# Four reorderings in a two-block gated cross-attention kernel: a weight subtraction on GpSimd, a context split and a set of bounds on VectorE, query copies on ScalarE

## The chip, the cores and the metric

The kernel runs on one core of a Trainium2 chip. The core has five engines that work side by side and wait for one another through semaphores: PE (TensorE, matrix products; PEld are its weight loads), DVE (VectorE), ACT (ScalarE), POOL (GpSimd) and SP (SyncE, which here issues nearly all DMAs). The metric is the device time of one execution in microseconds (us), as a median of several executions. Three executions of the kernel before gave 1867.23, 1867.36 and 1871.78 us, a median of 1867.36 us.

## The reference

Input are 4 sequences of 256 tokens by 256 features, `x`, and for each a context of 1601 rows by 128 features. Two layers follow one another, and each adds a gated cross-attention and a gated mixture of experts:

```
x = x + tanh(g_xattn[0]) * L0_xattn(layernorm(x), ctx)   # 16 heads of 16, layernorm on q and k, biases
x = x + tanh(g_ffn[0])   * L0_ffn(layernorm(x))          # 32 experts, top 8, capacity
x = x + tanh(g_xattn[1]) * L1_xattn(layernorm(x), ctx)   # 16 heads of 128, rmsnorm on q and k
x = x + tanh(g_ffn[1])   * L1_ffn(layernorm(x))          # 64 experts, top 4, router, 2 shared experts

# L1_xattn, for each batch element
q = rmsnorm(x @ Wq, gq); k = rmsnorm(ctx @ Wk, gk); v = ctx @ Wv      # heads of 128
out = softmax(q k^T / sqrt(128)) v;  out @ Wo
```

All is fp32. Products that need it are made from a high part, rounded to the fast fp32r format, and a low part, the exact remainder: three fast products (high-high, high-low, low-high) stand for one full one. So a tensor is often handled twice, as a "hi" copy (mostly ACT) and a "lo" subtraction (mostly DVE or POOL).

## The kernel before, in words

Every engine has its own instruction stream, written by hand in program order; nothing is reordered by a scheduler. An engine executes its stream strictly in order, and a wait holds everything behind it. `me.do(...)` makes an engine wait for its own instruction before the next; `.then_inc(s.name, 1)` raises a semaphore at the end and `wait_ge` waits for one. `primed(...)` only adds a constant.

The four stages are the first cross-attention (until about 380 us in the trace), the first experts (until about 610 us), the second cross-attention (until about 1545 us) and the second experts. The change touches the first and the third.

First cross-attention. Before the first scores, DVE scales the keys (L1778), makes the constants for the exponentials from the weights (`bounds()`, L1735 to L1741, six operations on a few columns, at whose end `bound0_ready` is raised), then subtracts the low parts of the first two key tiles (`read_keys(0, 0, 0)` and `(0, 0, 1)`, L1822), then turns to the first queries (`read_queries(0, 0)`, L1840 to L1845), and then to key tiles 2 and 3. After tile 1 it raises `kst_ready`, on which SP issues 12 DMAs of a first part of the keys (L604), and after tile 3 again, for 12 of the second part. PE waits for these DMAs before its first scores (L1235), and ACT for the scores and for `bound0_ready` before its first exponential (L972). POOL meanwhile works on L771, L775 and L778.

Second cross-attention. A preparation comes first: the products Wv Wo of all heads (PE L1394, `m1`), whose high parts ACT copies (L1022) and whose low parts are taken by POOL for heads 0 to 7 in one instruction over 2048 columns (L840, from the copy `m1w` that ACT makes in L1026) and by DVE for the rest (L2091). Beside it DVE normalizes x (L1665, eight tiles), PE turns the tiles (L449, "the token turn", `ln_turned`), ACT and DVE copy them out (L358, L1671), and PE goes on with the queries (L1420). POOL also clears the sums `rk1` and `acc1` (L842, L843), after the turn, and raises `sums_zeroed`.

Then come four batches (b = 0 to 3). Each has a key phase and a head phase. In the key phase the low part of the transposed context is subtracted on DVE over 1601 columns (L2103, `ctxT_lo`), while POOL subtracts and adds on the untransposed one (L856 to L861). PE makes the queries (L1420), then 52 key tiles in the order of `KINDS` ("k": L1404, squared by ACT in L1069, summed by DVE in L2131; "g": L1470, copied by ACT in L1073, weighted by POOL in L871, summed by DVE in L2131). PE may be four tiles ahead of ACT. DVE sums the squares of the queries (L2139, L2140), ACT takes the root behind the fourth tile (L1076), DVE inverts it (L2149), POOL scales the queries (L851, two instructions), and PE turns them (L1455) at the sixteenth tile. Between batches 1 and 2 the half of x that is finished is updated on DVE (`update`: L1962, L1638, L1641, and `variance`: L1652); this stands at the start of batch 2, ahead of L2103.

At the end of the key phase DVE finishes the sums of squares (L2163, `k1_var`), ACT takes their root (L1093) and loads the table of exponentials (L1094), DVE inverts (L2166, `rk1_ready`), and ACT begins the exponentials (L1112) of the first pair of heads. Around this stand the four high copies of the second query tile (ACT `split_products`, L1056) and their four low parts (DVE `low_products`, L2122): one copy ahead of the root, three behind the table load. Each pair of heads then runs over 13 context tiles: scores (PE L1404), exponentials (ACT L1112, two per tile), split (ACT L1120 or DVE L2206, then DVE L2210), sums (DVE L2219), values (PE L1404). PE may issue the scores of tile t once the exponentials of tile t-2 are done (t-3 for the first three).

## Time and profile before

| | |
|---|---|
| median of three executions | 1867.36 us (1867.23 to 1871.78) |
| profiled execution, own time | 1871.98 us |
| its span | 1870.2 us |
| busy in the span | PE 1785.2 us (95%), DVE 1403.3 us (75%), ACT 1231.6 us (66%), POOL 485.5 us (26%) |
| mean granted TensorE clock | 0.98 |
| busy PE, 380 to 400 us / 800 to 1500 us | 17.06 of 20 us / 684.60 of 700 us |

Times in the trace are counted from the start of the span. An engine's share of busy time tells little about what a change of order is worth; that is read from the places where an engine stands idle and from what ended the idle time. In a timeline row the columns are the start, the time from the first start to the last end of the merged instructions, the engine, the line, the operation, out<-in, the shape, the count, and in brackets the idle time before it and who ended it.

### The profile page before, as it was taken

To read this page: it belongs to the slowest core of one execution; us is meant where nothing else is said; L and a number is where in the kernel's file an instruction comes from. 1 tells how busy PE (TensorE), PEld (TensorE's weight loads), DVE (VectorE), ACT (ScalarE), POOL (GpSimd) and SP (SyncE) were. 2 spreads that over 40 slices of the span, in tenths; PEclk is the share of its full clock that TensorE was granted. 3 is DMA by queue.
4 is the path that set the end of the run, shared out by engine and by line. 5 is a ranking of instruction groups with operands and counts; after the bars stand their busy time and mean duration, and the time that the engine had idled before them with its cause. 6 is when DMAs were issued, how large, how long until landed. Compare 5 with 4: busy or idle time off the path is not lost.

```text
span 1870.2 us, 31883 instructions
## 1 busy us (share of the span) xinstructions
PE 1785.2 (95%) x9201; PEld 1309.9 (70%) x9204; DVE 1403.3 (75%) x2298; ACT 1231.6 (66%) x2094; POOL 485.5 (26%) x425
## 2 busy tenths in 40 slices
PE   5799999999999899999999989999999999999998
PEld 3344444468888667776777767777677777888887
DVE  7566666466666788887888989889789997566665
ACT  4576868842323688888888868888888885222322
POOL 3010101215453650005400054000530102445442
PEclk9899999989999999999999999999999999999999
DMA  3413222345443100000000000000000000554452
GB/s 99 111 46 83 67 62 59 70 175 127 118 111 77 54 18 1 0 0 18 18 1 0 0 18 19 0 0 0 1 22 1 8 9 17 116 116 109 109 116 75
DMA packets 109736, 95.90 MB, mean 51 GB/s; under 512 B 72820, under 2 KB 94200, under 8 KB 109016
## 3 DMA queue, kind: packets, MB, share of 16 engines
q1 hardware_dynamic: 109656, 94.88, 20.4%
q8 instruction: 45, 0.74, 0.2%
q14 instruction: 35, 0.29, 0.0%
HBM read 72.94 MB, written 1.44 MB: 40 GB/s over the span
## 4 chain that ended last, share of the span: by engine, by line
PE 81%; DVE 12%; ACT 3%; issue 2%; SPq 1%; DMA 0%; DVEq 0%; ACTq 0%
PE ps L1404 32%; PE ps L495 17%; PE ps L507 8%; PE ps L1248 5%; PE ps L1235 5%; DVE s_rk L2131 3%; PE ps L1173 3%; PE ps L1420 2%; PE ps L1498 1%; PE ps L1470 1%; PE ps L1526 1%; SPq L604 1%; DVE s_rq L2139 1%; ACT s_p L1112 1%; PE ps L1428 1%
## 5 line engine op out<-in xcount | busy, mean ns | idle before, releaser
L1112 ACT ACTIVATE s_p<-ps,s_g,s_rk 128x256 f32<-128x256 f32 (+1 forms) x832 | 412.5, 560 | 8.8 <-DVE s_dsum L2219 6.6
L1404 PE MATMUL ps<-s_qq,s_ctxT 128*128 (+3 forms) x1248 | 359.6, 402 | 9.6 <-ACT s_p L1112 7.8
L495 PE MATMUL ps<-s_xT,s_wgus 128*128 128x512 f32 x1440 | 348.5, 390 | 0.0
L1404 PE MATMUL ps<-s_ps,s_ctx 128*128 128x512 f32 x1152 | 327.4, 397 | 0.9 <-DVE s_ps L2210 0.9
L495 PEld LDWEIGHTS ps<-s_xT,s_wgus 128*128 128x128 f32 x1440 | 269.7, 188 | 59.6 <-issue 1.5
L2210 DVE TENSOR_TENSOR s_ps<-s_p,s_ps 128x512 fp32r<-128x512 f32 x384 | 269.0, 700 | 20.8 <-ACT s_ps L1120 17.4
L972 ACT ACTIVATE s_p<-ps,s_bsm 128x1024 f32<-128x1024 f32 x208 | 222.6, 1114 | 91.0 <-PE ps L1248 56.9
L1404 PEld LDWEIGHTS ps<-s_qq,s_ctxT 128*128 128x128 f32 (+1 forms) x1248 | 227.0, 186 | 68.2 <-issue 9.5
L1404 PEld LDWEIGHTS ps<-s_ps,s_ctx 128*128 128x128 f32 x1152 | 217.4, 189 | 57.5 <-DVE s_ps L2210 4.2
L2219 DVE TENSOR_TENSOR s_dsum<-s_dsum,s_p 128x512 f32<-128x512 f32 (+1 forms) x352 | 242.0, 687 | 16.5 <-ACT s_p L1112 12.9
L393 ACT CAST s_hs<-s_hw 128x512 fp32r<-128x512 f32 x120 | 74.5, 621 | 197.7 <-DVE s_hw L1995 197.7
L1120 ACT CAST s_ps<-s_p 128x512 fp32r<-128x512 f32 x288 | 179.4, 623 | 33.6 <-PE ps L1404 11.1
L2000 DVE TENSOR_TENSOR s_hs<-s_hw,s_hs 128x512 fp32r<-128x512 f32 x120 | 138.0, 1150 | 80.5 <-ACT s_hs L393 80.5
L507 PE MATMUL ps<-s_hs,s_wds 128*128 128x512 f32 x720 | 185.6, 393 | 1.8 <-DVE s_hs L2000 1.8
L387 ACT ACTIVATE s_sg<-ps 128x512 f32<-128x512 f32 x120 | 71.8, 599 | 145.6 <-PE ps L495 145.6
L1235 PE MATMUL ps<-s_qz,s_kT 96*128 96x512 f32 x416 | 148.1, 458 | 12.3 <-DMA s_kT<-s_kst 8.2
L507 PEld LDWEIGHTS ps<-s_hs,s_wds 128*128 128x128 f32 x720 | 134.7, 188 | 32.0 <-DVE s_hs L2000 2.6
L856 POOL TENSOR_TENSOR s_ctx<-s_stage,s_ctx 128x1536 fp32r<-128x1536 f32 x4 | 15.4, 3855 | 526.5 <-ACT s_ctxw L1039 526.5
L2131 DVE TENSOR_REDUCE s_rk<-s_ksq 128x4 f32<-128x512 f32 x208 | 128.3, 676 | 19.6 <-POOL s_ksq L871 16.4
L1991 DVE TENSOR_TENSOR s_hh<-s_sg,s_wB 128x512 f32<-128x512 f32 x112 | 77.6, 693 | 77.1 <-ACT s_sg L387 75.3
L1248 PE MATMUL ps<-s_p,s_vg 128*32 128x256 f32 x1792 | 126.2, 389 | 2.6 <-DVE s_oT L1850 2.6
L871 POOL TENSOR_TENSOR s_ksq<-s_ksq,s_stage 128x512 f32<-128x512 f32 (+1 forms) x104 | 111.4, 1091 | 35.2 <-ACT s_ksq L1073 34.6
(282 smaller groups left out, 2320.1 us busy)
## 6 DMA issues: line engine op xcount, KB each, us to landing
s_wB<-w1s SPq DMA_DIRECT2D x64, 256.0 KB, 3.9
s_kT<-s_kst SPq DMA_DIRECT2D x96, 128.0 KB, 2.4
s_kT<-s_kst SPq DMA_DIRECT2D x96, 80.0 KB, 2.1
s_wB<-w0s SPq DMA_DIRECT2D x15, 384.0 KB, 3.5
s_wB<-w0s SPq DMA_DIRECT2D x16, 256.0 KB, 3.8
s_wgu<-in_L_ffn_Wg_dram SPq DMA_DIRECT2D x64, 64.0 KB, 2.9
s_wgu<-in_L_ffn_Wu_dram SPq DMA_DIRECT2D x64, 64.0 KB, 2.6
s_wd<-in_L_ffn_Wd_dram SPq DMA_DIRECT2D x64, 64.0 KB, 2.5
```

The source lines that it names most:

```text
L495: ins = nc.tensor.matmul(ps[:, 4 + g, :], WGUS[f][:, slot, w, g, k, :], XT[f][:, x_, k, n], start=c == 0, stop=c == len(ops) - 1)
L507: ins = nc.tensor.matmul(ps[:, 2 * half + k, :], WDS[f][:, slot, w, k * P:(k + 1) * P], hs[:, j % 2, h, :], start=False, stop=False, skip_ ...
L972: nc.scalar.activation(p0[:, n % 4, :], ps[:, 2 * (n % 3):2 * (n % 3) + 2, :].rearrange("p a n -> p (a n)"), ACT.Exp, bias=bsm[:, col:col ...
L1112: ins = nc.scalar.activation(p1[0:r, SLOT1[t], j, :], ps[0:r, BANK1[t], j * SQ:(j + 1) * SQ], ACT.Exp, bias=g1[0:r, 3:4], scale=rk_col(t, ...
L1120: nc.scalar.copy(ps1[:, SPLIT1.index(t) % RING1, 0, :], p1[:, SLOT1[t], :, :].rearrange("p a n -> p (a n)")).then_inc(s.p_hi, 1)
L1235: ins = nc.tensor.matmul(ps[:, 2 * (n % 3) + i, :], kT0[0:32 * COPIES, g, i, t * P:(t + 1) * P], qz[0:32 * COPIES, g % 2, i, :], start=Tru ...
L1248: ins = nc.tensor.matmul(ps[32 * h:32 * h + 32, SUMBANK, dca * SQ:dca * SQ + SQ], vg[:, b % 2, t + dca, c:c + 2 * D0], p0[:, n % 4, h * SQ ...
L1404: ins = nc.tensor.matmul(out, lhs(x_), rhs(y_), start=first and n == 0, stop=last and n == 2)
L2000: v.tensor_tensor(hs[:, j % 2, 1, :], hw[:, j % 2, :], hs[:, j % 2, 0, :].bitcast(F32), ALU.subtract).then_inc(s.hs_lo, 1)
L2131: v.tensor_reduce(rk1[0:ROWS1[u], u, 4 * q:4 * q + 4], lengths(kind, i, u).rearrange("p (h d) -> p h d", h=4), AX, ALU.add).then_inc(s.k1_ ...
L2210: v.tensor_tensor(lo, whole(t), hi.bitcast(F32), ALU.subtract).then_inc(s.p_lo, 1)
L2219: v.tensor_tensor(dsum[0:r, :], dsum[0:r, :], whole(t)[0:r, :], ALU.add).then_inc(s.summed, 1)
```

## The change

On POOL, the subtraction over 2048 columns moves behind the wait for the token turn and the two memsets. On DVE, `bounds()` moves behind the first queries, and the context's low part moves ahead of the update and the variance (which concerns batch 2 alone, since the update is done there only). On ACT, two of the three late query copies move ahead of the root, and the last one behind the first pair of exponentials.

```diff
--- POOL
             g_.tensor_tensor(lo, whole, hi.bitcast(F32), ALU.subtract).then_inc(s.wk_lo, 1)
+            pool.wait_ge(s.ln_turned, 48)
+            me.do(g_.memset(rk1[:], 1.0))
+            g_.memset(acc1[:], 0.0).then_inc(s.sums_zeroed, 1)
             pool.wait_ge(s.m1_read, 4)
             n = slice(0, H1 * D // 2)
             g_.tensor_tensor(m1[:, 1, n], m1w[:], m1[:, 0, n].bitcast(F32), ALU.subtract).then_inc(s.m1_rest, 1)
-            pool.wait_ge(s.ln_turned, 48)
-            me.do(g_.memset(rk1[:], 1.0))
-            g_.memset(acc1[:], 0.0).then_inc(s.sums_zeroed, 1)
--- ACT
-                split_products(TB * b + 1, 0)
+                for j in range(3):
+                    split_products(TB * b + 1, j)
                 act.wait_ge(s.k1_var, b + 1)
                 nc.scalar.activation(rk1[:], rk1[:], ACT.Sqrt, scale=1.0 / D1).then_inc(s.k1_std, 1)
                 nc.scalar.activation(rq1[0:1, 1, 0:1], ones[0:1, 0:1], ACT.Exp).then_inc(s.act_steps, 1)
-                for j in range(1, 4):
-                    split_products(TB * b + 1, j)
...
                         ins.then_inc(s.probs1, 1)
+                        if t == 0 and first:
+                            split_products(TB * b + 1, 3)
--- DVE
             scale_keys(0, 1)
-            bounds()
             read_keys(0, 0, 0)
             read_keys(0, 0, 1)
             dve.wait_ge(s.kf_made, 4)
             dve.sem_inc(s.misc_read, 4)
             read_queries(0, 0)
+            bounds()
             read_keys(0, 0, 2)
...
             for b in range(B):
+                if b == 0:
+                    dve.wait_ge(s.sums_zeroed, 1)
+                else:
+                    dve.wait_ge(s.probs1, primed(KT * 8 * b))
+                dve.wait_ge(s.ctxT_hi, b + 1)
+                v.tensor_tensor(ctxT1[:, 1, 0:KV], stage[:, 0:KV], ctxT1[:, 0, 0:KV].bitcast(F32), ALU.subtract).then_inc(s.ctxT_lo, 1)
                 if b == B // 2:
                     update(acc1[:, 0:4, :].rearrange("p t n -> p (t n)"), 1, 0, 0)
                     variance(range(4))
-                if b == 0:
-                    dve.wait_ge(s.sums_zeroed, 1)
-                else:
-                    dve.wait_ge(s.probs1, primed(KT * 8 * b))
-                dve.wait_ge(s.ctxT_hi, b + 1)
-                v.tensor_tensor(ctxT1[:, 1, 0:KV], stage[:, 0:KV], ctxT1[:, 0, 0:KV].bitcast(F32), ALU.subtract).then_inc(s.ctxT_lo, 1)
```

POOL at the start of the second cross-attention, before and after; `s_m` is `m1`, `s_xn` the sums `acc1`, `s_ctx` the context. Lines shift by one or two in the changed kernel.

```order
L837 TENSOR_TENSOR s_wk<-s_stage,s_wk 128x2x512
L840 TENSOR_TENSOR s_m<-s_m1w,s_m 128x2048
L842 MEMSET s_rk 128x208
L843 MEMSET s_xn 128x2048
L856 TENSOR_TENSOR s_ctx<-s_stage,s_ctx 128x1536
```

```order
L837 TENSOR_TENSOR s_wk<-s_stage,s_wk 128x2x512
L839 MEMSET s_rk 128x208
L840 MEMSET s_xn 128x2048
L843 TENSOR_TENSOR s_m<-s_m1w,s_m 128x2048
L856 TENSOR_TENSOR s_ctx<-s_stage,s_ctx 128x1536
```

The wide subtraction now stands directly ahead of the context work.

ACT at the end of the key phase and the start of the first pair of heads (the same in each batch), before and after; `s_qq` are the query products, `s_rk` the key lengths, `s_p` the exponentials.

```order
L1056 CAST s_qq<-ps 128x4x128
L1093 ACTIVATE s_rk<-s_rk 128x208
L1094 ACT_TABLE_LOAD
L1094 ACTIVATE s_rq<-s_ones 1x1
L1056 CAST s_qq<-ps 128x4x128 x3
L1112 ACTIVATE s_p<-ps,s_g,s_rk 128x256 x2
L1120 CAST s_ps<-s_p 128x512
```

```order
L1056 CAST s_qq<-ps 128x4x128 x3
L1094 ACTIVATE s_rk<-s_rk 128x208
L1095 ACT_TABLE_LOAD
L1095 ACTIVATE s_rq<-s_ones 1x1
L1111 ACTIVATE s_p<-ps,s_g,s_rk 128x256 x2
L1056 CAST s_qq<-ps 128x4x128
L1121 CAST s_ps<-s_p 128x512
```

Two copies went ahead of the root, one behind the first exponentials.

DVE at the start of batch 2, before and after; `s_xn` are the sums, `s_x` is x, `s_ctxT` the transposed context.

```order
L2181 SCALAR_TENSOR_TENSOR s_xn<-ps,s_rd,s_xn 128x256 x4
L1962 SCALAR_TENSOR_TENSOR s_x<-s_xn,s_tg,s_x 128x1024
L1638 BN_STATS s_bn<-s_x 128x6 x4
L1641 BN_AGGR s_mv<-s_bn 128x2 x4
L1652 TENSOR_SCALAR s_lnv<-s_mv 128x4
L2103 TENSOR_TENSOR s_ctxT<-s_stage,s_ctxT 128x1601
L2139 TENSOR_REDUCE s_rq<-s_q1T 128x16
```

```order
L2182 SCALAR_TENSOR_TENSOR s_xn<-ps,s_rd,s_xn 128x256 x4
L2101 TENSOR_TENSOR s_ctxT<-s_stage,s_ctxT 128x1601
L1963 SCALAR_TENSOR_TENSOR s_x<-s_xn,s_tg,s_x 128x1024
L1639 BN_STATS s_bn<-s_x 128x6 x4
L1642 BN_AGGR s_mv<-s_bn 128x2 x4
L1653 TENSOR_SCALAR s_lnv<-s_mv 128x4
L2140 TENSOR_REDUCE s_rq<-s_q1T 128x16
```

The subtraction passed ten instructions of the update and the variance.

## Rows read from the trace of the kernel before

**Rows 1.** Page, part 4: shares of the chain that ended last, by engine
```profile
PE 81%; DVE 12%; ACT 3%; issue 2%; SPq 1%; DMA 0%; DVEq 0%; ACTq 0%
```

**Rows 2.** Timelines: preparation of the second cross-attention, and a normalization without POOL beside it
```profile
12.80 2.67 DVE L1665 TENSOR_SCALAR s_xn<-s_x,s_mv,s_lnv 128x256 f32<-128x256 f32 x8
...
618.04 4.61 DVE L1665 TENSOR_SCALAR s_xn<-s_x,s_mv,s_lnv 128x256 f32<-128x256 f32 x1
...
617.99 4.51 POOL L840 TENSOR_TENSOR s_m<-s_m1w,s_m 128x2048 fp32r<-128x2048 f32 x1 [7.11 <-ACT s_m1w L1026]
...
627.01 1.81 POOL L843 MEMSET s_xn<- 128x2048 f32 x1
...
623.35 3.27 PE L449 MATMUL ps<-s_ident,s_xn 128*128 128x128 f32 x16 [4.25 <-DVE s_xn L1665]
...
627.63 5.31 PE L1420 MATMUL ps<-s_wq,s_xnT 128*128 128x512 f32 x8 [1.02 <-DVE s_xnT L1671]
```

**Rows 3.** Windows: PE, PEld, DVE, ACT, POOL busy us, granted clock, DMA share, GB/s
```profile
624.00:631.00 7.00, 5.97 (x17) 3.33 (x15) 5.63 (x9) 4.36 (x6) 3.42 (x3) 0.51 0.00 0
...
921.00:924.50 3.50, 3.50 (x9) 2.69 (x9) 3.36 (x7) 3.33 (x8) 0.00 (x0) 0.51 0.03 7
...
1098.50:1102.00 3.50, 3.25 (x8) 2.57 (x9) 3.22 (x4) 0.88 (x2) 0.51 (x1) 0.51 0.59 203
```

**Rows 4.** Timelines of batch 0, key phase: POOL, DVE and ACT
```profile
635.26 3.45 POOL L860 TENSOR_TENSOR s_stage<-s_stage,s_ctx 128x1536 f32<-128x1536 f32 x1
...
637.80 0.94 DVE L2110 SCALAR_TENSOR_TENSOR s_g<-s_g 128x1 f32<-128x1 f32 x1
...
642.41 0.21 ACT L1076 ACTIVATE s_rq<-s_rq 128x16 f32<-128x16 f32 x1 [1.08 <-DVE s_rq L2140]
```

**Rows 5.** Timelines of batch 1, start: POOL and DVE
```profile
860.31 3.43 POOL L856 TENSOR_TENSOR s_ctx<-s_stage,s_ctx 128x1536 fp32r<-128x1536 f32 x1 [175.04 <-ACT s_ctxw L1039]
...
861.49 3.94 DVE L2103 TENSOR_TENSOR s_ctxT<-s_stage,s_ctxT 128x1601 fp32r<-128x1601 f32 x1
```

**Rows 6.** Timelines of batch 2, start: DVE, POOL, PE and ACT
```profile
1089.81 3.34 DVE L1962 SCALAR_TENSOR_TENSOR s_x<-s_xn,s_tg,s_x 128x1024 f32<-128x1024 f32 x1
...
1095.03 1.94 DVE L1652 TENSOR_SCALAR s_lnv<-s_mv 128x4 f32<-128x4 f32 x1
1096.89 1.81 DVE L2103 TENSOR_TENSOR s_ctxT<-s_stage,s_ctxT 128x1601 fp32r<-128x1601 f32 x1
1098.62 2.27 DVE L2139 TENSOR_REDUCE s_rq<-s_q1T 128x16 f32<-128x2048 f32 x1
...
1096.91 2.10 POOL L861 TENSOR_TENSOR s_stage<-s_stage,s_ctx 65x128 f32<-65x128 f32 x1
...
1098.76 2.93 PE L1404 MATMUL ps<-s_wk,s_ctxT 128*128 128x512 f32 x6 [4.08 <-DVE s_ctxT L2103]
...
1104.99 0.22 ACT L1076 ACTIVATE s_rq<-s_rq 128x16 f32<-128x16 f32 x1
```

**Rows 7.** Timelines of batch 1, start of the heads: ACT and PE
```profile
916.70 1.51 ACT L1056 CAST s_qq<-ps 128x512 fp32r<-128x512 f32 x3
918.11 1.00 ACT L1112 ACTIVATE s_p<-ps,s_g,s_rk 128x256 f32<-128x256 f32 x2
...
919.26 0.94 PE L1404 MATMUL ps<-s_qq,s_ctxT 128*128 128x512 f32 x3 [1.36 <-ACT s_p L1112]
920.79 2.71 PE L1404 MATMUL ps<-s_qq,s_ctxT 128*128 128x512 f32 x6 [0.59 <-ACT s_p L1112]
```

**Rows 8.** Timelines of the first cross-attention, start: DVE and SP's queue
```profile
44.08 1.53 DVE L1738 TENSOR_SCALAR s_bsm<-s_bsm 128x2 f32<-128x2 f32 x1
...
46.20 1.29 DVE L1822 TENSOR_TENSOR s_kst<-s_p,s_kst 128x512 fp32r<-128x512 f32 x2
...
65.21 0.81 DVE L1810 TENSOR_SCALAR s_kf<-ps,s_wcol 128x512 f32<-128x512 f32 x1 [2.78 <-DMA s_kT<-s_kst]
...
47.52 19.00 SPq L604 DMA_DIRECT2D s_kT<-s_kst  x28
```

More of the change, by code:

```diff
@@ L2092, in _ @@
             for b in range(B):
-                if b == B // 2:
-                    update(acc1[:, 0:4, :].rearrange("p t n -> p (t n)"), 1, 0, 0)
-                    variance(range(4))
                 if b == 0:
@@ L2103, in _ @@
                 v.tensor_tensor(ctxT1[:, 1, 0:KV], stage[:, 0:KV], ctxT1[:, 0, 0:KV].bitcast(F32), ALU.subtract).then_inc(s.ctxT_lo, 1)
+                if b == B // 2:
+                    update(acc1[:, 0:4, :].rearrange("p t n -> p (t n)"), 1, 0, 0)
+                    variance(range(4))
                 if b == 0:
```

## The prediction

> **What bounds the kernel now.** I read the page first. Four fifths of the chain that ended last are PE, an eighth is DVE [rows 1], so a change of order pays only where PE stands idle or where the work that feeds it is late. Then I took the timelines around the four places. At each the reader is to look for the bracket on PE's row, since its releaser says which engine to speed up, and for an instruction of odd length on that engine.
>
> At the preparation PE stands idle for 4.25 us for DVE's normalization, and the reason is one instruction: a tile that takes 4.61 us where eight take 2.67 us elsewhere, 0.33 us each. It starts with GpSimd's 2048-column subtraction (617.99 to 622.50) and ends with it, at 622.65 [rows 2]. Behind the gap TensorE's granted clock is at the lower of its levels, 1.2 GHz, for 7 us [rows 3]. The same blocking is seen in batch 0, where an operation on one column takes 0.94 us and ends with GpSimd's L860 [rows 4], and in batch 1, where the context subtraction (1.81 us alone) takes 3.94 us because L856 holds it up to 863.74 [rows 5, 6]. So: while GpSimd runs a wide subtraction, a DVE operation from SBUF to SBUF waits for its end. It goes both ways: GpSimd's 65-row L861 takes 2.10 us beside L2103 [rows 6].
>
> At batch 2 PE waits 4.08 us for L2103, which stands behind the update; clock at 0.51 from 1098.5 to 1102 [rows 3, 6]. At each start of the heads (four times; batch 1 stands for them) PE waits 1.36 and 0.59 us for exponentials that stand behind three query copies of 1.51 us, and the clock is at 0.51 behind that too [rows 3, 7]. In the first cross-attention SP issues 24 DMAs back to back from the moment `kst_ready` rises, and a DVE operation waits 2.78 us for the last of them [rows 8].
>
> **Part 1, the weight subtraction.** All instructions stay. Without it the eight tiles run 617.7 to 620.4 instead of to 624.6, 4.2 us sooner. PE is free at 619.1, turns, and is done at about 621.2; a copy of 0.69 us later the queries start, at 621.9 instead of 627.63. They also no longer fall into the half clock, which costs up to half of the 5.31 us that the first eight took less their normal share; I take 1.5 us. So PE comes to its first key tile about 7.2 us sooner, at 630.3. But that is not the gain. GpSimd now clears its sums (about 2.1 us with the 1.81 us row, to 623.3), then subtracts for 4.5 us to 627.8. L2103 asks for its turn at 624.3 and is held up until 627.8, ends at 629.5: still in time for PE. GpSimd's L856 (3.43 us) runs behind it to 632.9, L860 (3.45 us) from 633.7 to 637.2. DVE's small `g` operations run into both: the first is free at 632.9, the fourth at 637.2, the fifth behind L861 at 637.7. The query sum L2139 behind them (2.3 us) so ends at 640.1, and ACT's root is at 640.3 instead of 642.41 [rows 2, 4, 5]. ACT stands at that root behind the fourth key tile and PE may be four ahead: it does eight tiles by 635.6 and idles 5.5 us. So the lead is 2.1 us, and PE, which has no gap in the trace from there until 669 us, starts this stretch at half clock. At 3.5 to 7 us of half clock (the two lengths that rows 3 show) of which some passes while it idles, it loses 1.7 to 3.4 us. I take 1.8: **−0.3 us**, from −2.1 (no loss) to +1.3 (all of it).
>
> **Part 2, the third batch's context.** L2103 is asked for at 1089.8, is held up by L856 to 1092.06 (as L1962 was, whose 3.34 us are 2.25 of waiting and 1.1 of work) and ends at 1093.75. PE finds it ready when its queries end at 1094.1 instead of waiting to 1098.76. Behind it DVE does L1962 (1.1 us), the statistics (1.8 us) and L1652, which waits for L860 as before; GpSimd's L860 slips behind L1962 to about 1098.7. L2139 therefore starts at 1098.8, against 1098.62: DVE gains nothing here. But ACT, whose root before stood behind a late fourth tile and a table load of 1.28 us until 1104.99, now has its table loaded and only waits for L2140, at 1101.35: 3.6 us sooner [rows 6]. PE's gap moves too: 1099.4 to 1102.15, some 2.8 us, and a half clock of 3.5 us there costs 1.7 us in a stretch where PE is the bound. The queries scaled by GpSimd hang on DVE's inverse, which comes 2.1 to 2.4 us sooner, a second bound of the same size. **−2.0 us**, from −3.6 (no half clock) to 0 (L860 goes ahead of L1962, all 3.5 us of it).
>
> **Part 3, the bounds.** Before, DVE's constants stand ahead of the key tiles and wait for GpSimd (L1738, two columns, takes from 44.08 to 45.61; the two before it are held up in the same way). Now L1822 takes the first tile between two of GpSimd's operations; GpSimd's last ends at 45.6 plus the 0.65 us of that tile, 46.2, and the second tile is done at 46.85 instead of 47.49: 0.6 us, not 5. The 24 issues (19.00 us for 28, 0.68 each) start and end 0.6 us sooner, and with them the transfer that DVE waits for at 65.21. The bounds themselves are done at about 52.5 (six operations of under 0.2 us without GpSimd beside them, behind the queries at 51.4), before the first exponential could start, at 53.9. The second `kst_ready` comes 1.1 us later, at 53.4, while SP is busy with the first 12 DMAs until about 55. Cover is 1.4 us in both. **−0.6 us**, from −1.3 to 0 [rows 8].
>
> **Part 4, the query copies.** Four times. Before, three copies and the exponentials: 916.70 to 919.11. Two copies now run while ACT waits for DVE's sums, 1.25 us of idle time that hold two steps of 0.48 us, though PE delivers the second product only 0.1 us before the root is due: the root slips by 0.05 to 0.1 us. The exponentials of tile 0 start at 916.9 instead of 918.11, the copy behind them takes 0.5 us, and those of tile 1 start at 918.8 instead of 919.7: 0.9 us. PE waits for exactly these two, so its 1.36 us go nearly all and its second wait ends 0.9 us sooner; behind it there is no gap in the pair, so the 0.9 us count in full. What is queued behind DVE's wait for the last copy is the split of tile 0, for which ACT's cast is later still. **−3.6 us** for four, from −2.4 (0.6 each: PE at half clock is then the late one, not ACT) to −5.6 (1.4 each, if the shorter gap, 1.2 us instead of 1.95, no longer brings the half clock) [rows 3, 7].
>
> **The sum.** −0.3 −2.0 −0.6 −3.6 = −6.5 us. Against the profiled execution's own 1871.98 us that is 1865.5; it stands 4.6 us over the median of the runs, which ones with the same program also spread over (1867.23 to 1871.78). From the median: **1860.9 us**.
>
> **A rule beside it.** The trace shows that a DVE instruction that already waits gets its turn ahead of GpSimd's next one: L1652 and L2103 both ran before L861 [rows 6]. The Trainium skill ("SBUF — State Buffer", "SBUF: two separate sides") says that the pair of ports shared by the two is an exclusive lock, held for a whole instruction by whichever starts first. It does not say who starts first when both wait; if GpSimd did, the sum would be that of the last rival below. Its rule that a two-input DVE operation is held up only by a GpSimd operation that reads SBUF leaves the memsets harmless, as I have them. The skill also states ("TensorE: Matmul & The Clock Gate", "Part 1: The HAM clock gate") that the monitor of TensorE's activity runs free of the kernel's start; no row here shows that, and by it each half clock would be a matter of luck from run to run, between the ends given above.
>
> **The rivals.**
> - *The clock comes back as well.* At the heads the shorter gaps keep the clock at 2.4 GHz, and the moved gaps of parts 1 and 2 cost nothing: −2.1 −3.0 −0.6 −5.6 = −11.3 us, 1856.1. For it: the gap at the heads shrinks by 0.8 us. Against it: all four gaps of 1.95 us cost the clock, and those of parts 1 and 2 are longer. 12%.
> - *Only part.* PE, at half clock behind each start of the heads, is later than ACT anyway and takes 0.3 us from part 4, and DVE's chain gives batch 2 only 1 us: −0.3 −1.0 −0.6 −1.2 = −3.1 us, 1864.3. For it: the first six products behind the second wait take 2.71 us, with no gap. 22%.
> - *The long gap costs more than the lead.* Part 1 pays 3.4 us of half clock for 2.1 us, and part 2 nothing: +1.3 +0 −0.6 −2.4 = −1.7 us, 1865.7: no change that can be told. 8%.
> - *GpSimd keeps the port: slower.* If GpSimd's next instruction starts ahead of a waiting DVE one, L2103 of batch 0 waits behind L840, L856, L857 and L860, to 637.2, and ends at 639: PE starts its key tiles at 639 instead of 637.6, after a gap of 9 us and at half clock for 7 us, +1.4 +3.5 us = +4.9. Batch 2 gains nothing; with L1962 also late, +1. With −0.6 and −2.4 of the rest: +2.9 us, 1870.3. It decides from the point where two of GpSimd's wide ones run back to back over a waiting L2103. Against it: L861 in batch 2. 6%.
> - The forecast has 52%.
>
> **Range and chances.** Three runs of 1867 us tell 0.3%, 5.6 us, from no change; below 1861.8 is faster, above 1873.0 slower. The forecast's own range is 1858 to 1864; its lower seven tenths lie below 1861.8, which with the first rival gives 0.50. To hold 8 in 10 the range takes in the second and third rival and most of the first: 1856.5 to 1866.0. Same: 0.45, and slower, the last rival with a run in a poor place, 0.05.
>
> **What would show it.** Right: no tile of L1665 over 0.5 us at 618; L840's successor between the memsets and L856; PE's gap gone at 619 and a new one of 4 to 6 us after eight key tiles of batch 0; the root at 2 us, not 7, before its old place. In batch 2, no wait of L1404 for L2103. At the heads a wait of PE of about 1.2 us instead of 1.95. Wrong: L2103 of batch 0 ending after 631, PE waiting for it, ACT waiting for the bounds before its first exponential, or the root of the key phase more than 0.2 us later than the sums. If the clock is at 0.5 for less of the changed kernel than before, the time lies below the range.

## The result, and the profile after

The changed kernel took 1856.17 us (median of six, 1854.01 to 1856.77) against 1867.8 us for the kernel before on the same chip (six, 1866.3 to 1871.78). The ratio is 0.9926, 95% interval 0.9913 to 0.9938: faster, by 11.6 us by the medians and by 13.8 us by the ratio (11.6 to 16.2). The forecast was −6.5 us, 1860.9, with a range of 1856.5 to 1866.0. Its direction was right, its size about half of what came, and the time lies 0.3 us below the range. The profiled execution took 1856.43 us, with a span of 1854.7 us at a mean granted clock of 0.988, where before it was 0.984.

The page of the changed kernel, parts 1 and 4, says little of this. PE's busy time fell by 4.5 us, and the rest of the 15.5 us between the two spans is idle time that went. The chain of part 4 could be followed back over 42% of the span only, against 99% before, so the two can't be compared.

```profile
PE 1780.7 (96%) x9204; PEld 1303.2 (70%) x9204; DVE 1401.1 (76%) x2298; ACT 1232.0 (66%) x2094; POOL 485.1 (26%) x425
...
PE 36%; DVE 4%; ACT 1%; issue 1%; DVEq 0%; ACTq 0%
```

Where the time went is read from the places of the change. The preparation and batch 0's key phase after the change, by timelines of POOL, DVE, ACT and PE (they answer to [rows 2, 4]):

```profile
621.45 4.53 POOL L843 TENSOR_TENSOR s_m<-s_m1w,s_m 128x2048 fp32r<-128x2048 f32 x1
625.94 5.07 POOL L856 TENSOR_TENSOR s_ctx<-s_stage,s_ctx 128x1536 fp32r<-128x1536 f32 x1
...
631.50 3.50 POOL L860 TENSOR_TENSOR s_stage<-s_stage,s_ctx 128x1536 f32<-128x1536 f32 x1
...
615.47 2.68 DVE L1666 TENSOR_SCALAR s_xn<-s_x,s_mv,s_lnv 128x256 f32<-128x256 f32 x8
...
622.33 5.33 DVE L2101 TENSOR_TENSOR s_ctxT<-s_stage,s_ctxT 128x1601 fp32r<-128x1601 f32 x1
...
628.80 2.23 DVE L2111 SCALAR_TENSOR_TENSOR s_g<-s_g 128x1 f32<-128x1 f32 x1
...
631.93 0.16 DVE L2115 TENSOR_SCALAR s_g<-s_g 128x1 f32<-128x1 f32 x1
632.12 0.15 DVE L2116 TENSOR_SCALAR s_g<-s_g 128x1 f32<-128x1 f32 x1
632.19 2.27 DVE L2140 TENSOR_REDUCE s_rq<-s_q1T 128x16 f32<-128x2048 f32 x1
...
635.06 0.21 ACT L1076 ACTIVATE s_rq<-s_rq 128x16 f32<-128x16 f32 x1 [2.72 <-DVE s_rq L2141]
...
635.80 0.95 PE L1405 MATMUL ps<-s_wk,s_ctxT 128*128 128x512 f32 x3 [1.55 <-ACT s_ksq L1073]
```

The eight tiles run in 2.68 us as forecast, L2101 is held up until L843's end and is still in time, L2111 until L856's end. Then comes what was not forecast: two operations on one column, L2115 and L2116, run in 0.16 and 0.15 us while L860 runs from 631.50 to 635.00. From the start of the tiles to the root it is 635.06 − 615.47 = 19.59 us, where it was 642.41 − 617.72 = 24.69 before: 5.10 us less, where 2.1 were forecast. PE's new gap is 1.55 us, not 5.5.

Two operations with one input and more columns were held up in the same kernel, by this L860 and by that of batch 2 (which ended at 635.00 and at 1087.90); before, the first of them took 0.18 us with no operation of GpSimd beside it:

```profile
634.50 0.53 DVE L2141 TENSOR_SCALAR s_rq<-s_rq 128x16 f32<-128x16 f32 x1
...
1086.43 1.49 DVE L1653 TENSOR_SCALAR s_lnv<-s_mv 128x4 f32<-128x4 f32 x1
```

Batch 2 [rows 6] and the start of batch 1's heads [rows 7] after the change:

```profile
1079.99 3.15 DVE L2101 TENSOR_TENSOR s_ctxT<-s_stage,s_ctxT 128x1601 fp32r<-128x1601 f32 x1
1083.07 1.47 DVE L1963 SCALAR_TENSOR_TENSOR s_x<-s_xn,s_tg,s_x 128x1024 f32<-128x1024 f32 x1
...
1077.81 7.89 PE L1421 MATMUL ps<-s_wq,s_xnT 128*128 128x512 f32 x16
1085.14 1.95 PE L1405 MATMUL ps<-s_wk,s_ctxT 128*128 128x512 f32 x6
...
1091.19 0.95 PE L1405 MATMUL ps<-s_wk,s_ctxT 128*128 128x512 f32 x3 [0.40 <-ACT s_ksq L1073]
...
1090.36 0.21 ACT L1076 ACTIVATE s_rq<-s_rq 128x16 f32<-128x16 f32 x1 [0.17 <-DVE s_rq L2141]
...
907.66 1.02 ACT L1111 ACTIVATE s_p<-ps,s_g,s_rk 128x256 f32<-128x256 f32 x2
908.57 0.58 ACT L1056 CAST s_qq<-ps 128x512 fp32r<-128x512 f32 x1
...
910.65 1.89 PE L1405 MATMUL ps<-s_qq,s_ctxT 128*128 128x512 f32 x6 [0.89 <-ACT s_p L1111]
```

PE's wait of 4.08 us is gone, and at the heads 1.36 and 0.59 us have become 0.89 us (and 0.21 us of issue). The six products behind it take 1.89 us instead of 2.71: they run at 2.4 GHz. The clock is read from the windows of the changed kernel (columns as in [rows 3]):

```profile
618.00:645.00 27.00, 24.26 (x118) 17.44 (x119) 23.64 (x31) 19.66 (x36) 24.97 (x15) 1.00 0.10 31
676.00:690.00 14.00, 12.77 (x65) 9.22 (x64) 12.89 (x21) 13.39 (x27) 1.09 (x1) 1.00 0.21 59
1074.50:1081.50 7.00, 6.39 (x23) 4.25 (x24) 4.04 (x7) 4.37 (x7) 3.47 (x2) 0.76 0.00 1
1533.00:1537.50 4.50, 4.44 (x22) 3.71 (x22) 2.95 (x7) 0.58 (x1) 0.00 (x0) 0.62 0.00 0
```

From the start of the second cross-attention on, the trace before had six stretches at 1.2 GHz (6.8 us at the preparation, 3.4 us behind each of the four starts of the heads and in batch 2's gap). This one has two, of 3.4 us, and both in places that were undisturbed before: at the end of batch 1 (1076.3) and of batch 3 (1533.7).

Taken from place to place, the lead of this trace over the one before is 2.25 us at the tiles of the preparation (of which 1.06 us were there before the first place of the change), 6.0 us more by PE's second wait at the heads of batch 0, then 1.9, 4.3 and 2.1 us more by the same wait of batches 1, 2 and 3. From there to the end of the stage 0.9 us of it are lost again.

### The profile page after: what moved, and what is told of

Read it like the earlier page. It is cut to its first block and busy times, and to the rows that moved or that the text cites. A ratio compares the mean times of both kernels' runs of the same rounds, so it can differ in the third digit from the quotient of the medians.

```text
span 1854.7 us, 31886 instructions
## 1 busy us (share of the span) xinstructions
PE 1780.7 (96%) x9204; PEld 1303.2 (70%) x9204; DVE 1401.1 (76%) x2298; ACT 1232.0 (66%) x2094; POOL 485.1 (26%) x425
## 5 line engine op out<-in xcount | busy, mean ns | idle before, releaser
L1405 PEld LDWEIGHTS ps<-s_qq,s_ctxT 128*128 128x128 f32 (+1 forms) x1248 | 222.8, 184 | 68.4 <-ACT s_p L1111 12.0
L2220 DVE TENSOR_TENSOR s_dsum<-s_dsum,s_p 128x512 f32<-128x512 f32 (+1 forms) x352 | 241.9, 687 | 16.2 <-ACT s_p L1111 12.7
L856 POOL TENSOR_TENSOR s_ctx<-s_stage,s_ctx 128x1536 fp32r<-128x1536 f32 x4 | 15.4, 3847 | 520.5 <-ACT s_ctxw L1039 520.5
L1236 PEld LDWEIGHTS ps<-s_qz,s_kT 96*128 96x128 f32 x416 | 69.6, 193 | 70.7 <-issue 48.3
```

The lines of the kernel that those rows point to most:

```text
L1236: ins = nc.tensor.matmul(ps[:, 2 * (n % 3) + i, :], kT0[0:32 * COPIES, g, i, t * P:(t + 1) * P], qz[0:32 * COPIES, g % 2, i, :], start=Tru ...
L1405: ins = nc.tensor.matmul(out, lhs(x_), rhs(y_), start=first and n == 0, stop=last and n == 2)
L2220: v.tensor_tensor(dsum[0:r, :], dsum[0:r, :], whole(t)[0:r, :], ALU.add).then_inc(s.summed, 1)
```

## The experiments

Twelve kernels ran, in three groups; each group has its own runs of the kernel before, and a ratio in us is taken of 1868 us. The twelfth, with an operation on 127 columns, ran once (1860.66 us, in the group of the last three), for its trace, and gives no ratio. "Clock" is the mean granted clock over the runs of a kernel.

| kernel | runs | median, us | before, us (runs) | ratio to before, 95% | in us | clock |
|---|---|---|---|---|---|---|
| part 1 alone | 12 | 1864.98 | 1868.55 (35) | 0.9971 [0.9961, 0.9982] | −5.4 | 0.986 |
| part 2 alone | 12 | 1867.52 | the same | 0.9994 [0.9984, 1.0004] | −1.1 | 0.983 |
| part 3 alone | 12 | 1868.91 | the same | 0.9997 [0.9985, 1.0008] | −0.6 | 0.984 |
| part 4 alone | 12 | 1865.81 | the same | 0.9978 [0.9969, 0.9988] | −4.1 | 0.984 |
| all but part 1 | 5 | 1863.62 | 1872.57 (9) | 0.9956 [0.9943, 0.9970] | −8.2 | 0.986 |
| two columns | 5 | 1865.15 | the same | 0.9964 [0.9950, 0.9977] | −6.7 | 0.985 |
| sums first | 5 | 1858.80 | the same | 0.9926 [0.9912, 0.9939] | −13.8 | 0.988 |
| late exponentials | 5 | 1861.96 | the same | 0.9940 [0.9926, 0.9954] | −11.2 | 0.987 |
| the whole, again | 5 | 1855.51 | 1869.37 (9) | 0.9925 [0.9912, 0.9939] | −14.0 | 0.988 |
| last copy later | 5 | 1856.02 | the same | 0.9933 [0.9920, 0.9947] | −12.5 | 0.989 |
| all but part 4 | 5 | 1858.82 | the same | 0.9952 [0.9939, 0.9966] | −9.0 | 0.987 |

The kernel before had a clock of 0.983 over the 35 runs of the first group, the changed one 0.989 over its first six.

### Each part alone

Each of the four is the kernel before with one part of the diff above: part 1 its first block (POOL), part 4 the block of ACT, part 3 the move of `bounds()`, part 2 the move of the context's subtraction.

> The kernel before with part 1 alone: GpSimd's 2048-column weight subtraction behind the token turn and the two memsets. Theory R (read from the changed kernel's trace, where the root of the key phase comes 5.1 us ahead of the 2.0 us of lead that existed before it, and PE's gap behind eight key tiles is 1.55 us at full clock): -5 us, -4 to -6, root at about 637.3, no lower clock from 620 to 640. Theory F (the forecast on record: small operations held up by both of GpSimd's, a gap of 5.5 us and 1.8 us lost to the clock): -0.3 us, -2.1 to +1.3. Theory G (the lead is given back at the exponentials or the next batch): lead of 5 us at the root, but -1 to -3 in the time.

Root and first gap of part 1 alone, from its timelines, and its window:

```profile
637.39 0.21 ACT L1076 ACTIVATE s_rq<-s_rq 128x16 f32<-128x16 f32 x1 [2.70 <-DVE s_rq L2140]
...
638.14 0.95 PE L1404 MATMUL ps<-s_wk,s_ctxT 128*128 128x512 f32 x3 [1.53 <-ACT s_ksq L1073]
...
618.00:645.00 27.00, 24.23 (x113) 16.78 (x112) 23.64 (x34) 20.32 (x39) 22.62 (x12) 1.00 0.09 32
```

Its tiles start at 617.81, so the root comes 19.58 us behind them, as in the whole. Part 1 gave −5.4 us (−7.3 to −3.4), theory R; the forecast's −0.3 lies outside, and so do its bound of −2.1 and theory G's −1 to −3. The lead arrives at the heads too: from the start of the tiles to the first exponentials of batch 0 it is 66.67 us, against 71.81 before, 5.1 less.

> The kernel before with part 2 alone: the third batch's context subtraction ahead of update and variance. Theory R (in the changed kernel the lead grows by 2.9 us across batch 2's key phase, after a lower clock that came with it): -3 us, -2.4 to -4.2; PE's wait of 4.08 us gone, a wait of about 0.4 us at its ninth key tile. Forecast on record: -2.0 us (-3.6 to 0), with a gap of 2.8 us at the ninth tile and 1.7 us lost at half clock.

```profile
1093.33 1.96 PE L1404 MATMUL ps<-s_wk,s_ctxT 128*128 128x512 f32 x6
...
1101.04 1.37 PE L1404 MATMUL ps<-s_wk,s_ctxT 128*128 128x512 f32 x3 [2.05 <-ACT s_ksq L1073]
...
1100.20 0.21 ACT L1076 ACTIVATE s_rq<-s_rq 128x16 f32<-128x16 f32 x1 [1.82 <-DVE s_rq L2140]
```

PE does not wait for the context any more. It waits 2.05 us at its ninth tile instead (forecast: 2.8), and the three products behind that gap take 1.37 us, half of them at half clock. From the last sums of batch 1 (DVE, 1087.14) to PE's turn of the queries (1106.63) it is 19.49 us, against 1109.84 − 1087.91 = 21.93 before: 2.4 us. Of that the runs show −1.1 us (−3.0 to +0.7). That is the picture of the forecast, and its −2.0 us lies inside. In the whole the same stretch is 1095.28 − 1078.12 = 17.16 us, 4.8 us less than before: there PE reaches its ninth tile later, since its queries take 7.89 us at partly half clock, waits 0.40 us, and the clock stays up. But these 4.8 us do not all arrive. From the first exponentials of batch 1 to those of batch 2, part 2 gives 2.3 us alone (235.45 before, 233.14), and 2.25 to 2.43 us in three more pairs of traces that differ there by part 2: part 1 alone and all but part 4, part 4 alone and the changed kernel, part 4 alone and all but part 1. A fifth pair gives 1.5 us; its first trace, that of part 3 alone, has its half clocks at other places.

> The kernel before with part 3 alone: the bounds behind the first queries. Theory R (the lead grew by 1.1 us from 40 to 75 us in the changed kernel): -1.1 us. Forecast on record: -0.6 us (-1.3 to 0). Rival: the 1.1 us are a matter of the first DMAs of an execution, not of the order: 0 us.

−0.6 us (−2.8 to +1.5): the forecast's number, but the runs can't tell it from nothing. The traces can, over a short stretch: from GpSimd's L771 to PE's first scores, before and in the changed kernel,

```profile
38.43 1.82 POOL L771 TENSOR_TENSOR s_qn<-s_qn,s_s 128x512 f32<-128x512 f32 x1 [25.68 <-DVE s_s L1787]
...
53.26 3.75 PE L1235 MATMUL ps<-s_qz,s_kT 96*128 96x512 f32 x8 [8.19 <-DMA s_kT<-s_kst]
```

```profile
37.37 1.82 POOL L771 TENSOR_TENSOR s_qn<-s_qn,s_s 128x512 f32<-128x512 f32 x1 [24.63 <-DVE s_s L1788]
...
51.26 3.75 PE L1236 MATMUL ps<-s_qz,s_kT 96*128 96x512 f32 x8 [7.25 <-DMA s_kT<-s_kst]
```

it is 14.83 and 13.89 us. In the four traces without part 3 it is 14.81 to 14.83, in the ten with it 13.86 to 13.93: part 3 brings the scores, and the first exponentials behind them, 0.9 us sooner. Whether that arrives at the end is not shown. The trace of part 3 alone shows something else as well. The order of its heads is that of before, with the same waits, and yet the clock is at 1.00 behind them (680 to 700 us and 908 to 930 us); the half clock stands at the end of batch 0 instead:

```profile
680.00:700.00 20.00, 17.83 (x88) 13.29 (x87) 18.03 (x30) 18.11 (x36) 1.09 (x1) 1.00 0.15 41
854.00:858.00 4.00, 4.00 (x15) 3.06 (x15) 1.46 (x4) 2.15 (x4) 1.77 (x1) 0.57 0.00 0
```

So the two waits of 1.36 and 0.60 us do not bring the half clock each time, and the place in a batch at which it comes differs from one trace to another.

> The kernel before with part 4 alone: the query copies, in all four batches. Theory R (the lead grows by 1.45 to 1.5 us at each of the four starts of the heads, about 0.9 by the order and 0.5 since the clock stays up): -6 us, or -4.4 where a lower clock comes at the end of the stage instead, as in the changed kernel's trace. Forecast on record: -3.6 us (-2.4 to -5.6). Rival (only the order counts, the clock falls anyway): 4 x 0.9 = -3.6 us with the granted clock at 0.5 behind each start.

−4.1 us (−5.8 to −2.2), between the forecast's −3.6 and theory R. The waits are those of the whole (0.89 us at all four starts). In its trace the clock does not fall behind the starts of the heads but at 854.3, 1315.0 and 1543.7, at the ends of batches 0, 2 and 3. So the rival, by which it falls at the heads anyway, is wrong, but the half clocks have moved more than gone: from 600 us to the end of this stage the trace has 23.8 us at half clock, as many as the one before, and the mean clock of the runs is 0.984 against 0.983.

### Taking one part out

Part 1 is taken out of the changed kernel by putting GpSimd's lines back behind the subtraction (only the removed lines are shown), part 4 by putting ACT's copies back in the same way.

```diff
-            pool.wait_ge(s.ln_turned, 48)
-            me.do(g_.memset(rk1[:], 1.0))
-            g_.memset(acc1[:], 0.0).then_inc(s.sums_zeroed, 1)
```

> The changed kernel without part 1 (parts 2, 3 and 4 on the kernel before). Parts add: the four alone gave -5.4, -1.1, -0.6 and -4.1 us by their ratios, so this is -5.8 us against the kernel before, 1863. Rival (the parts share a loss at the clock, which ends only when nearly all of its places are gone): less than -5.8, about -4, since the whole gave -13.8 by its ratio where the parts sum to -11.2.

> The changed kernel without part 4 (parts 1, 2 and 3 on the kernel before). Parts add: +4.1 us against the changed kernel, as part 4 alone gave -4.1 us. By the trace's leads (1.5 us at each start of the heads): +6 us. Rival (only the order counts, 0.9 us each, the forecast's term): +3.6 us.

Without part 1 the gain is 8.2 us instead of 13.8 to 14.0, so it is worth 5.7 us there and 5.4 alone; the gain is more than either theory had (5.8 and about 4), with 5.8 inside the interval of 5.6 to 10.6. By the stretch from the tiles to the first exponentials part 1 is worth 5.1 to 5.7 us in four pairs of traces. Without part 4 it is 9.0 us, so part 4 is worth 5.0 us there and 4.1 alone, where 4.1, 6 and 3.6 were expected, and the runs can't choose among the three. The parts alone sum to −11.2 us, the whole has −13.8 and −14.0; the intervals, of some 2 us each, leave open whether there is more in the whole. In the trace without part 4, PE's waits at the heads are back, in batch 0 at full clock and in batch 1 at half clock:

```profile
683.26 1.87 PE L1404 MATMUL ps<-s_qq,s_ctxT 128*128 128x512 f32 x6 [0.60 <-ACT s_p L1112]
...
910.95 2.87 PE L1404 MATMUL ps<-s_qq,s_ctxT 128*128 128x512 f32 x6 [0.60 <-ACT s_p L1112]
```

Against the trace of the changed kernel (median of the differences between the starts of like instructions) batch 0's start costs 0.85 us and batch 1's 1.5 us. So the order is worth 0.85 us at each start, as forecast (0.9), and a half clock there another 0.65.

All traces of this case together say more on the clock than any one of them. In the five kernels without part 4 it fell behind 12 of 20 starts of the heads, in eight with it behind none of 32 (and behind 2 of 4 in the one with late exponentials, below). At the ends of the batches it was the other way: 4 of 20 without part 4 (all four in the trace of part 3 alone), 17 of 32 with it. The time from the first exponentials of batch 0 to those of batch 1, and of 2 to 3, gives the prices:

| | intervals | us | mean |
|---|---|---|---|
| without part 4, no half clock | 4 | 227.4 to 228.1 | 227.7 |
| without part 4, one behind the heads | 4 | 228.2 to 228.7 | 228.5 |
| with part 4, no half clock | 7 | 226.7 to 227.3 | 226.9 |
| with part 4, one at the end of the batch | 7 | 227.8 to 228.5 | 228.1 |

The order is worth 0.8 us a batch, a half clock behind the heads costs 0.8 us, and one at the end of a batch 1.2. So the shorter wait does keep the clock up at the heads, but part of that is paid back at the ends, at a higher price.

### The step of part 1 that failed

The forecast had DVE's small operations held up by L860. An operation more, on two columns, ahead of the two that passed, and the same on 127 columns:

```diff
                     me.do(v.tensor_tensor(g1r[:, 2, :], g1r[:, 0, :], g1r[:, 1, :], ALU.mult))
+                    me.do(v.tensor_scalar(g1r[:, 2, 0:2], g1r[:, 2, 0:2], 1.0, 0.0, ALU.mult, ALU.add))
                     me.do(v.tensor_reduce(g1[:, 3:4], g1r[:, 2, :], AX, ALU.max, apply_absolute_value=True))
```

> The changed kernel with one more DVE operation on two columns of a 128-column tile (times 1, plus 0) ahead of the two small operations that ran while GpSimd's L860 did (631.93 and 632.12, 0.16 and 0.15 us). Theory C (a one-input operation on one column of fp32 needs nothing that the two engines share, one on two or more columns does): it starts at about 631.7, is held up until L860's end at 635.0, 3.3 us, the query sum starts at 635.5 and the root stands at 637.9 instead of 635.06; PE's gap behind eight key tiles is 4.4 us instead of 1.55, and the time +2.9 us by the order alone, +4.6 with 1.7 us of half clock behind the gap, as the forecast had for such a gap. Theory N (L860 at that moment lets any small operation of one input pass): 0.2 us, +0.2 us in all.

> As the kernel with the two-column operation, with 127 columns instead of two. Theory C (every one-input operation on more than one column is held up by L860): about 3.4 us for it. Theory E (an odd number of fp32 columns goes without what the two engines share, an even one doesn't): 0.3 us, not held up, and the root as in the changed kernel, about 0.3 us later.

With two columns, DVE, POOL, ACT and PE:

```profile
631.27 3.41 DVE L2114 TENSOR_SCALAR s_g1r<-s_g1r 128x2 f32<-128x2 f32 x1
...
631.17 3.49 POOL L860 TENSOR_TENSOR s_stage<-s_stage,s_ctx 128x1536 f32<-128x1536 f32 x1
...
637.81 0.22 ACT L1076 ACTIVATE s_rq<-s_rq 128x16 f32<-128x16 f32 x1 [5.81 <-DVE s_rq L2142]
...
638.55 1.65 PE L1405 MATMUL ps<-s_wk,s_ctxT 128*128 128x512 f32 x3 [4.65 <-ACT s_ksq L1073]
...
638.50:642.50 4.00, 3.94 (x10) 3.17 (x11) 3.53 (x7) 3.48 (x7) 2.71 (x2) 0.57 0.00 0
```

With 127 columns:

```profile
629.54 3.47 DVE L2114 TENSOR_SCALAR s_g1r<-s_g1r 128x127 f32<-128x127 f32 x1
```

So theory C holds: the two-column one takes 3.41 us and ends with L860, the one-column ones take 0.15. An odd number of columns is no way out (3.47 us): it is the single column. (The added operation works on another tile than the one-column ones, with the arithmetic of the first of them; a single column of that tile was not tried.) The tiles of this execution start at 615.13, so the root is 22.68 us behind them, 3.09 more than in the changed kernel. PE's gap grows from 1.55 to 4.65 us, and behind it the clock falls for 3.4 us, from 638.7. PE's turn of the queries comes 4.5 us later (644.13 − 615.13 against 639.98 − 615.47), so 3.1 by the order and 1.4 by the clock. The forecast took 1.8 us for the clock there: nearly the right price, for a gap that the kernel doesn't have. In the time the operation costs 7.1 us by the ratios (0.9964 against 0.9926), with some 3.5 us to either side; from the tiles to the first exponentials of batch 0 it is 69.84 us against 65.47, 4.4 us. Expected were 4.6.

### A try at the rest of the gap, and at the heads

All small operations (five; the expectation counts seven) behind the first query sum, and L860 of batch 0 behind it too (POOL's side of the edit; DVE's, the move itself, is left out):

```diff
+                if b == 0:
+                    pool.wait_ge(s.q1_var, 1)
                 me.did(g_.tensor_tensor(st[:, full, :], st[:, full, :], ctx1[:, 1, full].bitcast(F32), ALU.add))
```

> The changed kernel with the seven small operations on g behind the first query sum and its mean, and GpSimd's L860 of batch 0 behind that mean too. Theory C (one-column or not, every wide operation of GpSimd that stands beside DVE's chain to the root costs): the query sum starts at 630.4, when ACT's last square is done, the mean at 632.7 finds GpSimd idle, root at 632.9 instead of 635.06, PE's gap of 1.55 us gone; -1.5 us, since PE was the bound until then. Rival: GpSimd's products, now 1.4 us later, take its place at the tiles that it weighs: 0 us, or +0.5 us.

```profile
632.90 0.22 ACT L1078 ACTIVATE s_rq<-s_rq 128x16 f32<-128x16 f32 x1 [0.51 <-DVE s_rq L2135]
...
633.03 3.58 POOL L862 TENSOR_TENSOR s_stage<-s_stage,s_ctx 128x1536 f32<-128x1536 f32 x1 [1.57 <-DVE s_rq L2135]
...
640.10 1.09 PE L1458 MATMUL ps<-s_ident,s_p 128*128 128x128 f32 x8 [1.04 <-POOL s_p L851]
641.96 1.09 PE L1458 MATMUL ps<-s_ident,s_p 128*128 128x128 f32 x8 [0.76 <-POOL s_p L851]
```

The root came 2.2 us sooner and PE's 1.55 us went, as forecast, but 1.8 us of waits for GpSimd's scaled queries took their place. The ratio is the changed kernel's, 0.9926, so the rival holds. GpSimd, 26% busy over the whole, is what PE waits for in these ten microseconds.

Eight one-element exponentials ahead of the first wide one:

```diff
                 nc.scalar.activation(rq1[0:1, 1, 0:1], ones[0:1, 0:1], ACT.Exp).then_inc(s.act_steps, 1)
+                for k in range(1, 9):
+                    nc.scalar.activation(rq1[0:1, 1, k:k + 1], ones[0:1, 0:1], ACT.Exp)
```

> The changed kernel with eight one-element exponentials ahead of the first wide one in each batch, which takes the start of the heads 1.0 to 1.6 us back, so that PE's gap of 0.88 us is about as long as the 1.95 us of before. Theory G (the gap at the heads decides on the clock there): four half clocks of 3.4 us behind the starts come back, and the time is 4 x (delay + 0.5) = +6 to +8.4 us, time at half clock +13 us. Theory P (the half clocks in this stage come once in a batch whatever the gap, at one place or another): 4 x delay = +4 to +6.4 us, time at half clock unchanged.

They took 0.84 us, so the gap is 1.63 us. In batch 0 the clock stayed up behind it and the delay cost 0.5 us; in batches 1 and 3 it fell (913.2 and 1374.0, 3.4 us each) and cost 1.1 us. Two of four: neither theory as it was put. The time is +2.6 us by the ratios (0.9940 against 0.9926, with some 3.5 us to either side), less than either had (6 to 8.4, and 4 to 6.4). In batch 0:

```profile
683.21 0.93 PE L1407 MATMUL ps<-s_qq,s_ctxT 128*128 128x512 f32 x3 [0.76 <-ACT s_p L1113]
685.01 1.86 PE L1407 MATMUL ps<-s_qq,s_ctxT 128*128 128x512 f32 x6 [0.87 <-ACT s_p L1113]
```

Last, the fourth copy two tiles later on ACT, and its low part on DVE (only ACT's side of the edit is shown):

```diff
-                        if t == 0 and first:
+                        if t == 2 and first:
                             split_products(TB * b + 1, 3)
```

> The changed kernel with the fourth query copy (ACT) behind the exponentials of tile 2 instead of tile 0, and its low part (DVE) behind the split of tile 2. Theory A (PE's remaining 0.88 us at the heads hang on that copy of 0.48 us, which stands ahead of tile 1's exponentials): the gap is 0.40 us, and the time -1.9 us against the changed kernel, 4 x 0.48. Rival (ACT has no idle time in the first pair, so the copy costs the same 0.48 us two tiles later): 0 us, with a gap of 0.4 us at the same place and another one of up to 0.5 us behind it.

```profile
683.86 1.88 PE L1405 MATMUL ps<-s_qq,s_ctxT 128*128 128x512 f32 x6 [0.61 <-ACT s_p L1111]
...
686.68 0.96 PE L1405 MATMUL ps<-s_qq,s_ctxT 128*128 128x512 f32 x3 [0.26 <-ACT s_p L1111]
```

0.61 and 0.26 us in place of 0.88: the wait was cut in two (in batch 1 it stayed at 0.89, with 0.26 behind it), and the ratio, 0.9933, is not better than 0.9925. So the rival holds here too, and none of these versions beat the changed kernel.

## Why the prediction was right or wrong

- **Part 1, −0.3 us forecast, −5.4 measured.** This is the step that failed, in the words of the forecast: "DVE's small `g` operations run into both: the first is free at 632.9, the fourth at 637.2, the fifth behind L861 at 637.7.". The first was held up. The fourth and fifth were not, as they work on one column with one input. What I took as evidence, L2110 in [rows 4], has one column but two inputs, and L1652 in [rows 6] has one input but four columns. The trace before has no one-input operation on one column beside a wide one of GpSimd, so the cost should have been bounded from both sides, 0.2 us and 3.4 us; the bound of −2.1 left out the lower end. The step is worth 3.1 us of order, and with the gap of 4.65 us that it makes, 1.4 us of clock (the two-column kernel). Together that is 4.5 of the 5.1 us by which the part was missed, and the part is 5.1 of the 7.3 us by which the sum was missed (by the ratio). Behind the step stands a rule drawn too widely, "a DVE operation from SBUF to SBUF waits for its end": besides the single columns the reduction over 2048 columns, L2140, ran beside L860 in 2.27 us, as at its other places. The steps ahead of it were right: the tiles, L2101 in time, the pace of POOL.
- **Part 2, −2.0 forecast, −1.1 (−3.0 to +0.7) alone.** Right, with its new gap and its half clock, and right in the whole too: from heads to heads it is 2.3 to 2.4 us there, though the stretch of the key phase alone gains 4.8.
- **Part 3, −0.6 forecast, −0.6 (−2.8 to +1.5).** Not resolved by the runs; by the traces 0.9 us up to the first scores. Its steps are in the trace of the changed kernel: the bounds take 0.15 to 0.23 us each (50.35 to 51.55), and the first exponentials start at 52.54, behind PE's first scores at 51.26. The second key tile, L1823 at 44.10, takes 1.42 us, where two later ones take 0.89 together (51.58), so part of the blocking stayed.
- **Part 4, −3.6 forecast, −4.1 alone and −5.0 in the whole.** Right for the order, 0.8 to 0.85 us against 0.9. Its other end, −5.6 with the clock up, is not far from the whole either; the runs can't tell the two apart.
- **The clock.** I charged the two new gaps with 3.5 us and gave nothing back elsewhere. It was the other way: over the runs the time at half clock, 2 × (1 − clock) × span, fell from 62 to 42 us. Over the 35 runs of the kernel before, a least-squares line gives 0.27 us for a microsecond of it, so some 5 of the 13.8 us would be the clock's; that is a slope over scattered runs, and no experiment shows it. The intervals leave less room: 5.1 to 5.7 for part 1, 2.3 to 2.4 for part 2, 0.9 for part 3 and four times 0.8 for part 4 make 11.5 to 12.2 us, what each stretch's own clock costs or saves included for the first two. The forecast's last sign, a time below the range if the clock is at 0.5 for less of the changed kernel, did come true. The first rival, at 1856.1, had that and was given 12%. It named the right time by luck, as it had not the mechanism of part 1: it too had the root 2.1 us sooner.
- **GpSimd keeps the port.** It didn't: L2101 had been waiting since 622.33 when L843 ended at 625.98 and L856 was next. L2101 ran first, and L856 took 5.07 us instead of 3.43, longer by L2101's 1.7. This holds in part 1 alone and in the two-column kernel too.
- **The rule on the lock.** The trace of the changed kernel shows one-input operations on 4 and 16 columns held up (1.49 us for L1653, 0.53 for L2141), the experiments those on 2 and 127 (3.41 and 3.47), and a single column not (0.16). The Trainium skill ("SBUF — State Buffer", "SBUF: two separate sides") has the pair of ports taken by a DVE operation in a two-port mode as well as by one with two inputs from SBUF; its page "VectorE: DVE Perf Modes" ("What auto-detection actually checks") grants that mode to one source in SBUF whose outermost dimension of more than one element is even, or equal in source and destination. The runs agree: 127 is odd and equal, and a single column has no such dimension, though the page does not say what comes of that. That the mode is the reason was not measured; the runs show only which forms are held up. I had weighed the first page and not asked which of the small operations fall under it.

What stays open: whether the whole has more than the sum of its parts (2.6 us by the ratios, with an uncertainty as large), and why the clock, where the wait at the heads is short, falls at the end of one batch and not of the next.

## What to carry to other kernels

A small operation on VectorE's critical path beside a wide one of GpSimd cost as much as GpSimd's had left to run where it had two inputs or more than one column, and nothing where it had one input and one column or was a reduction; before counting on either, look for a row of exactly that form, and where there is none keep both ends of the range. Sum the clock like any other term, and with both signs: here a half clock cost 0.65 to 0.8 us behind a start of the heads, 1.2 us at the end of a batch and 1.4 us behind the gap of the two-column kernel, on top of the gap itself, and the forecast charged the new gaps while giving nothing back for those that shrank. Where the runs can't resolve a part, a short interval between two rows of the same trace may: part 3's 0.9 us repeated within 0.1 us over fourteen traces whose times differ by up to 16 us. An engine that is busy for a quarter of the time can be the bound for ten microseconds, and a copy moved off one wait can make the next.

## What the runs showed of the hardware

- One column of fp32 with one input beside a wide operation of GpSimd (L860, an addition): 0.15 and 0.16 us; two columns 3.41 us; 127 columns 3.47 us. One column with two inputs, beside the subtraction L856: 2.23 us. Reductions from 128 columns to one and from 2048 to 16, beside L860: 0.29 us, as without it, and 2.27 us, as at its other places.
- The granted clock fell to 1.2 GHz in stretches of 3.4 us also where the waits just ahead were of 0.23 to 0.24 and 0.61 us (1076.3 and 1533.7 in the changed kernel, 854 in that with part 3 alone), and it stayed at 2.4 GHz behind waits of 1.36 and 0.60 us at 8 of 20 starts of the heads, among them batch 0 of three kernels (parts 1 and 3 alone, all but part 4). With part 4, where that wait is a single one of 0.6 to 0.9 us, it never fell there (32 starts). Behind a gap of 4.65 and 4.68 us it fell, in both kernels that had one.
- The same kernel spread over 7.7 us in 35 runs (1865.71 to 1873.37), the changed one over 2.8 us in six.
